# A memset behind the last operation carries the signal of VectorE's rounds in decoding, records and wide rows

## The reference

```
h   = relu(layernorm(x))
h   = h @ W                                   # 8192 x 128
s_src, s_dst = h @ a[:128], h @ a[128:]
e   = leaky_relu(s_src[:, None] + s_dst[None, :], 0.2)
e   = where(adj > 0, e, -9e15)
out = x + softmax(e, axis=1) @ h
```

## Time and profile before

| | us |
|---|---|
| median of 3 runs | 855.32 (850.54 to 856.79) |
| the profiled execution | 856.59 |
| its span, from the first to the last instruction | 854.8 |
| VectorE busy | 584.7 (68%), 3117 instructions |
| ScalarE busy | 532.1 (62%) |
| GpSimd busy | 508.9 (60%) |
| TensorE busy, matmuls | 456.6 (53%) |
| DMA | 299.31 MB, mean 350 GB/s |

### The profile page before, as it was taken

One profiled execution on the slowest core, in us unless ns is written; L12 is line 12 of the kernel. 1 busy time (PEld: TensorE's weight loads), 2 busy tenths in 40 slices (PEclk: granted clock), 3 DMA queues, 4 the chain that ended last, 5 costly groups with the idle time before them and its releaser, 6 DMA issues.

```text
span 854.8 us, 8934 instructions
## 1 busy us (share of the span) xinstructions
PE 456.6 (53%) x1823; PEld 217.7 (25%) x1855; DVE 584.7 (68%) x3117; ACT 532.1 (62%) x375; POOL 508.9 (60%) x522
## 2 busy tenths in 40 slices
PE   4685666556655547634556555565155655534321
PEld 3551223222222213212222222232022222212221
DVE  7817567766677667646778676777277788756784
ACT  3998667667677676756396666767272977732000
POOL 3725666656656665765655666666666666665571
PEclk9999658776667777757776777778577868765555
DMA  8989999999999999989699999999698799992110
GB/s 341 415 302 420 406 407 410 408 410 409 409 410 408 409 407 405 405 345 394 254 378 406 408 409 408 411 392 410 231 390 333 283 406 411 410 399 73 25 38 11
DMA packets 40903, 299.31 MB, mean 350 GB/s; under 512 B 11052, under 2 KB 14034, under 8 KB 24464
## 3 DMA queue, kind: packets, MB, share of 16 engines
q1 hardware_dynamic: 22976, 276.83, 79.7%
q0 software_dynamic: 15328, 17.58, 6.6%
q10 hardware_dynamic: 2544, 4.33, 1.5%
HBM read 304.31 MB, written 8.65 MB: 366 GB/s over the span
## 4 chain that ended last, share of the span: by engine, by line
DVE 71%; another core or an unknown queue 11%; issue 10%; PE 3%; ACT 2%; DMA 2%; SPq 0%; POOLq 0%; DVEq 0%; ACTq 0%
DVE x_all L806 19%; DVE rest L623 6%; DVE words L621 5%; DVE words L625 5%; DMA adj_buf<-in_adj 2%; DVE wf L651 2%; DVE top_bit L647 2%; DVE top L665 1%; DVE one_hot L753 1%; DVE cand L661 1%; DVE e L770 1%; DVE cand L708 1%; PE banks L1034 1%; DVE rec L729 1%
## 5 line engine op out<-in xcount | busy, mean ns | idle before, releaser
L359 POOL DMA_INDIRECT gathered<-table,index x448 | 448.5, 1001 | 291.7 <-DVE index L699 148.0
L465 ACT ACTIVATE mask_buf<-adj_buf,minus_half 128x2048 bf16<-128x2048 int32 x256 | 497.2, 1992 | 138.6 <-DMA adj_buf<-in_adj 52.7
L1034 PE MATMUL banks<-mask_buf,bit_ident 128*128 128x512 bf16 x992 | 327.9, 485 | 44.1 <-issue 27.0
L1034 PEld LDWEIGHTS banks<-mask_buf,bit_ident 128*128 128x128 bf16 x1024 | 115.2, 124 | 217.4 <-issue 153.1
L806 DVE SCALAR_TENSOR_TENSOR x_all<-gathered,weight,x_all 128x128 f32<-128x128 f32 x512 | 157.5, 348 | 14.2 <-DVE x_all L806 6.5
L1046 PE MATMUL banks<-is_wide,before 128*128 128x1 bf16 x64 | 6.8, 176 | 181.7 <-DVE is_wide L736 151.2
L479 ACT ACTIVATE prob<-e 128x16 f32<-128x16 f32 x31 | 6.5, 208 | 102.3 <-issue 68.3
L1075 PE MATMUL banks<-x_all,one_hot 128*128 128x128 f32 x128 | 35.8, 373 | 61.5 <-issue 42.3
L621 DVE MAX8 words<-banks 128x8 f32<-128x512 f32 x64 | 44.4, 693 | 18.7 <-PE banks L1034 9.7
L1046 PEld LDWEIGHTS banks<-is_wide,before 128*128 128x128 bf16 x64 | 4.5, 112 | 201.8 <-DVE is_wide L736 167.0
L625 DVE MAX8 words<-rest 128x8 f32<-128x512 f32 x64 | 44.5, 695 | 3.5 <-issue 0.7
(11 more groups left out here) (160 smaller groups left out, 581.1 us busy)
## 6 DMA issues: line engine op xcount, KB each, us to landing
adj_buf<-in_adj SPq DMA_DIRECT2D x128, 2048.0 KB
gathered<-table,index POOLq DMA_INDIRECT x448
table<-gathered ACTq DMA_DIRECT2D x4, 1040.0 KB, 9.3
x_all<-in_x SPq DMA_DIRECT2D x3, 1024.0 KB, 10.5
out<-x_all SPq DMA_DIRECT2D x2, 1280.0 KB
x_all<-in_x SPq DMA_DIRECT2D x2, 512.0 KB, 5.2
out<-x_all SPq DMA_DIRECT2D x1, 1024.0 KB
w_gathered<-table,w_index POOLq DMA_INDIRECT x24
```

What stands on the lines that cost most here:

```text
L359: nc.gpsimd.indirect_dma_start(g_cols[buf][:, k, :], None, table, bass.IndirectOffsetOnAxis(index[:, buf, k:k + 1], 0), bounds_check=N, oo ...
L465: nc.scalar.activation(mask_buf[:, u], adj_buf[:, u], ACT.Sign, bias=minus_half[:]).then_inc(mask_ready, 1)
L1034: ins = mm(bank, bit_ident[:, h * PART_BITS + c], mask_buf[:, u, c * BIT_COLS:(c + 1) * BIT_COLS], start=False, stop=(h == PARTS - 1 and c ...
```

## The change

A helper `fenced` is added. It runs one step of `beside`, then a memset of the one-column `fence` that carries the signal, then waits:

```diff
+            def fenced(beside=iter(())):
+
+                next(beside, None)
+                done.add(v.memset(fence[:], 0.0))
+                settled()
```

In `decode`, `make_records`, the first two rounds of `weighted_sum`, and in `wide_index`, `wide_logits` and `wide_sum`, the round's last operation loses its signal, and `settled()` and `next(beside, None)` become `fenced(beside)`, or `fenced()` where nothing runs beside. All places are of these kinds:

```diff
@@ decode
                 v.tensor_scalar(unfit[:, 0, B], words[:, B, WIDE - 1], ...)
-                done.add(v.tensor_scalar(wi[0][:, B], words[:, B], float(BIT_COLS), None, ALU.mult))
-                settled()
-                next(beside, None)
+                v.tensor_scalar(wi[0][:, B], words[:, B], float(BIT_COLS), None, ALU.mult)
+                fenced(beside)
...
                 for b in range(lo, hi):
-                    ins = v.match_replace(cand[:, b], top[:, b, 0:8], cand[:, b], 0.0)
-                done.add(ins)
-                settled()
+                    v.match_replace(cand[:, b], top[:, b, 0:8], cand[:, b], 0.0)
+                fenced()
...
                 for _ in beside:
-                    done.add(v.memset(fence[:], 0.0))
-                    settled()
+                    fenced()
@@ make_records
-                done.add(v.tensor_scalar(rec[:, ring, :, REC_NODE], node0[:], ...))
-                settled()
+                v.tensor_scalar(rec[:, ring, :, REC_NODE], node0[:], ...)
+                fenced()
@@ weighted_sum
-                next(beside, None)
-                done.add(v.tensor_reduce(l4, prob[:, two, B], AX.X, ALU.add))
-                settled()
-                next(beside, None)
-                done.add(v.reciprocal(r4[:, B], l4))
-                settled()
-                next(beside, None)
+                v.tensor_reduce(l4, prob[:, two, B], AX.X, ALU.add)
+                fenced(beside)
+                v.reciprocal(r4[:, B], l4)
+                fenced(beside)
                 done.add(v.tensor_tensor(weight[:, B], prob[:, two, B], ...))
@@ wide_sum (wide_index and wide_logits alike)
-                done.add(v.tensor_reduce(w_m[:, 1:2], w_prob[:], AX.X, ALU.add))
-                settled()
+                v.tensor_reduce(w_m[:, 1:2], w_prob[:], AX.X, ALU.add)
+                fenced()
```

## The result

| | us |
|---|---|
| median before, 4 runs | 856.06 (850.54 to 860.54) |
| median after, 4 runs | 884.82 (883.26 to 885.76) |
| after to before | 1.0318, 95% interval 1.0273 to 1.0363 |

The kernel became 28.8 us slower; the forecast was 859.0 in a range of 850 to 867. Ratios here leave out runs that took over 1.5% more than the fastest of their kernel; where too few are left, there is only a median with the range of the runs.

A forecast was written before the change was run, and what follows sets the result against it. VectorE's fixed-order work was taken to bound the kernel. Of 609 added memsets, 30 early and 130 late ones were hidden; the rest at 8 ns gave 3.6 us, so median 855.32 became 859, range 850 to 867.

The forecast's parts named there:

- VectorE does not set when these are let go, so there 8 ns earlier or later is mostly swallowed: At VectorE's rounds waiting for late signals, the memset's 8 ns was counted as nothing.
- 130 late rounds: Waits, 131 in the list, behind late signals that move to a memset; left out of the sum as swallowed.
- the forecast had 3.6 us: Sum over VectorE's rounds: (609 - 30 - 130) x 8 ns; 4.9 us if nothing is swallowed.
- the forecast's overlap: In undisturbed VectorE rounds the memset starts about 0.06 us before its predecessor ends, so its 59 ns isn't added whole.
- its 8 ns: Cost of one memset per undisturbed VectorE round, from 42 ns a round with and 33 ns without; 2 to 15 possible.
- 450 memsets and lengthened rounds: The VectorE rounds counted as paying 8 ns, after leaving out 30 early ones and 130 behind late signals.
- the rival of a signal that is not held back: At VectorE's late signals, a one-column memset may signal sooner; prize 120.9 us, floor about 820 us; chance 0.13.
- The rival of the late softmax: `logits_ready` in `weighted_sum` comes 0.60 us later, holding back masks, banks and VectorE: 8.4 us, 864 us; chance 0.08.
- The rival of memsets that don't overlap: Behind decode's other forms and in full rounds, each memset costs 59 ns: 26.6 us, 882 us; chance 0.07.
- The idle time that should have stayed at 121 us: Sign: VectorE's idle time before L646, L650, L655 and L660 of decode stays about 121 us in all.
- the 891 us worked out from the rule: By the skill's DRAIN rule every VectorE memset costs 59 ns whole: 609 x 59 ns = 36 us.

The follow-up runs named there:

- f3: Kernel before plus sixteen one-column memsets without a signal at the head of round L655, inside the held-back stretch; 874.02 us beside 850.20, ratio 1.0301.
- f2: The kernel after, unchanged, traced on the same chip as the kernel before; 863.70 us beside 850.20, ratio 1.0194.
- e1: Kernel before with all 609 memsets added, each step beside still behind the wait; 885.02 us beside 860.42, ratio 1.0288.
- f4: Kernel before plus sixteen memsets without a signal at the head of round L706, behind `index`, outside the stretch; 884.81 us (862.71 to 887.01).
- e8: Kernel before with 439 of the 609 memsets, none in decode's five rounds L642, L646, L650, L655, L660, steps behind the wait; 873.86 us beside 856.99, 1.0180.
- e3: Kernel before with the change in `weighted_sum` alone, 66 memsets; 865.44 us beside 860.42, ratio 1.0042.
- e6: Kernel after with ten gathers a batch in place of fourteen; 813.02 us beside 856.99 for the kernel before, ratio 0.9477.
- e5: Kernel before with ten gathers a batch in place of fourteen; 802.78 us beside 856.99, ratio 0.9367.
- e12: Kernel before with GpSimd waiting for a batch's first ten gathers to land before issuing the eleventh; 899.31 us beside 852.33, ratio 1.0608.
- g1: Kernel before with GpSimd waiting for a batch's first five gathers to land before the eighth; 879.12 us beside 860.09, ratio 1.0240.
- e4: Kernel before with the steps of `place_wide` begun four rounds later, no memset added; 858.22 us beside 860.42, ratio 0.9958.
- e9: Kernel before with `place_wide` ten rounds later in batches 0 to 30, `add_records` behind the fourth `pack`; 867.40 us beside 852.33, ratio 1.0079.
- f1: The kernel before, unchanged, traced on the same chip as the kernel after; 850.20 us beside 850.20, ratio 1.0019.

## Why the prediction was wrong

**The step that failed** is "VectorE does not set when these are let go, so there 8 ns earlier or later is mostly swallowed". The rows for it were two signals let go together and the list of late waits. I read the late waits as a delay of the signals, with a fixed end. They are more of a rate: VectorE is let on in steps of 0.7 us there, usually one instruction each in the short rounds, and memsets without a signal are held in the same steps (`f3`). So the term that the forecast put at nothing, 130 late rounds with their memsets swallowed, is where most of the loss arises: within the stretch VectorE starts 10.9 operations of a batch before and 5.9 after (the 14 batches of above). The steps can be read from the trace of before: its rounds in the stretch take 1.41 us with two instructions and 2.13 with three in the median, and I looked only at how long the waits were and at the kind of operation in front.

**The size.** Per batch the places don't add up to 0.7 us each. The stretch ends about 2 us behind the last gather whatever VectorE does, and what is pushed behind it runs at full speed. Nor do the memsets' own places explain all: 2.8 memsets stand in the stretch of a batch after, and 5.0 fewer operations pass it. What is left of a batch's memsets is 0.72 us in the first pair of traces and 1.05 us in the pair of one chip. The first makes 21.6 us over 30 batches and, with 1.1 us ahead of them and 6.5 behind, 29.2 us of span (854.8 to 884.0), where the forecast had 3.6 us.

**What was right.** The instructions are 609 more, a memset lasts 59 ns, and in an undisturbed round it overlaps. In order of time, the kernel after:

```profile
429.89 0.17 DVE L658 TENSOR_SCALAR top_bit<-wf 128x32 int32<-128x32 int32 x1
430.01 0.06 DVE L538 MEMSET fence<- 128x1 f32 x1
430.11 0.19 DVE L660 TENSOR_TENSOR wf<-wf,top_bit 128x32 f32<-128x32 f32 x1
```

It starts 0.05 us before the operation in front ends, and the next round 0.05 us behind that end. So the forecast's overlap holds, and its 8 ns lie within the rounding of these starts. Busy time rose by 3.7 us, 6 ns for each of the 609; that the forecast's sum is 3.6 us is chance, for it counts 450 memsets and lengthened rounds. The memset's signals are held like others (1.22 us at 510.72 in `f2`), so the rival of a signal that is not held back fell. The rival of the late softmax fell with `e1`, which leaves the logits' steps where they were and costs as much. The rival of memsets that don't overlap came nearest in time, 882 us, by luck: it is wrong, the rows above overlap. The idle time that should have stayed at 121 us is 103.0 us on the same four lines (27.6 + 35.7 + 20.5 + 19.2; the last two below) and 55.7 us on the line in front of them, L642 of before, which had next to none.

```profile
L660 DVE TENSOR_TENSOR wf<-wf,top_bit 128x32 f32<-128x32 f32 (+1 forms) x34 | 6.5, 191 | 19.2 <-remote 14.9 <-issue 1.8 <-DVE fence L538 1.5
...
L656 DVE TENSOR_SCALAR cand<-cand 128x2 f32<-128x2 f32 (+1 forms) x34 | 5.8, 172 | 20.5 <-remote 12.4 <-DVE fence L538 5.0 <-issue 2.5
```

The rule of the Trainium skill that the prediction cites, page "VectorE: DVE Perf Modes", section "The DRAIN you can't avoid", was read there as if it held for every operation. The same section goes on to say that an operation that is not held (in the page's own sense of the word) starts earlier than the emptying of the pipe, and the trace agrees with that: sixteen memsets take 0.22 us together in `f4`, where sixteen times 59 ns are 0.94 us. So the 891 us worked out from the rule are near to 884.8 by chance.

**What stays open.** That the kernel after falls behind in the stretch is shown; how memsets that stand outside the five rounds bring a loss about (38 ns each in `e8`, and 5.0 us for 66 of them in `e3`) is argued only: a later arrival at the stretch lets fewer rounds slip through before it. In the two kernels on one chip, of the rounds that ended between 13.25 and 13.5 us behind the first gather, 4 of 17 were followed over 0.15 us late before, and L642's round, on time there in the rows above, takes 1.40 us after. No run sets that arrival alone. The 10.2 us left with ten gathers (`e6`) may come from the holding back that is left there. Nor is it settled what in GpSimd's gathers holds VectorE: fewer gathers (`e5`) and a wait for the first ten landings (`e12`) take most of it away, a wait for the first five (`g1`) doesn't. Each run's clock and span come from records of its instructions, so no run shows whether VectorE is held without them.

## What to carry to other kernels

When an engine's waits for its own signals are long, sort such rounds by their number of instructions before calling it latency: where the time goes up with that number, the engine is let on at a rate, and an added instruction can cost there, also one that nobody waits for. Look then at what the other engines do in that window. (Moving five instructions out of it was tried here and won at most 0.4%, `e4` and `e9`.) And compare two kernels batch by batch on one chip: behind totals that scatter by 2% stood a steady 1 us a batch, and single stalls of 10 us in one of the traces.

## What the runs showed of the hardware that was not expected

Beside the last of 14 gathers that GpSimd issued in a row, VectorE was let on in steps of 0.7 us, also with memsets that carry no signal (`f3`), and ran at full speed from about 2 us behind the end of the last; ScalarE's signals came on time there (0.06 us). With 28 in a row it waited up to 8.3 us at one place (`f1`). Where GpSimd had waited in each batch for the first ten landings, VectorE was not held in nine rows of 14, though it worked beside their last gathers (`e12`). Where the holding back sets in differed between two traced executions of the kernel before: of the rounds that ended 13.25 to 13.5 us behind the first gather, 13 of 18 were followed late in the first (22.82 us a batch) and 4 of 17 in `f1` (21.98). Whether that hangs on the chip or on the execution isn't shown.
